# A decoder megakernel: the windowed attention's softmax in five plan steps instead of one

## The chip, the cores and the metric

The kernel is one program on one core of a Trainium2 chip. The metric is the device time of one execution in microseconds; lower is better.

## What is computed

The reference runs six blocks over x of 4 x 512 tokens with 256 channels: a time-mixing block, a quantised cross-attention, a mixture of experts, linear attention, cross-attention, and last a local-attention transformer of two layers. Only the last one's attention is touched. Cut to what matters:

```python
def _layer(x, wqkv, qs, ksc, wo, ...):
    qkv = shift_token(x) @ wqkv
    q, k, v = ...                      # 8 heads of 64
    q, k = rotary_xpos(l2norm(q) * qs, l2norm(k) * ksc)
    o = local_attention(q, k, v)       # a block of 128 queries sees its own
    x = x + o @ wo                     # and the previous block's 128 keys
    ...                                # then a gated feed-forward part

def local_attention(q, k, v):
    sim = einsum('bhwid,bhwjd->bhwij', bq * 8.0, bk)
    sim = where(mask, -max, sim)
    return einsum('bhwij,bhwjd->bhwid', softmax(sim), bv)
```

## The kernel before, in words

The tokens are 16 tiles of 128, four to a sequence. The windowed attention (`windowed_attention`) runs once per layer over 8 units of two tiles (u = 0 to 7, w = 0 or 1). One list of steps, `windowed_plan`, sets the order of the work: each engine's function (`attention_pe`, `attention_dve`, `attention_act`, `attention_pool`) walks the same list and issues its own part of each step, so the list gives the order in every engine's queue. Semaphores order the engines among each other. A step is named by kind, unit, tile, and for some the part.

For a tile the steps are: `project` (three products with the weights for queries, keys and values on TensorE, L3297; ScalarE empties the bank, L3505, and after the keys squares both, L3511; VectorE sums the squares, L3405), `split` (VectorE copies the shifted channels, L3396, ScalarE casts, L3493 and L3495, GpSimd subtracts, L3567; it prepares the input of a later unit's projections), `rotate` (VectorE L3422 and L3425 with GpSimd L3578 and L3579), `scale` (VectorE L3433, by the inverted norms), `invert` (ScalarE's square root L3515, VectorE L3409 and L3411), `turn` (TensorE's transposes L3306, ScalarE's copies L3524 for keys, L3529 for queries), `score` (L3318 writes the mask, L3325 the products, four banks for 8 heads), `softmax`, `flip` (transposes L3337 of the weights; ScalarE and VectorE copy one half each, L3480), `combine` (L3352, copied by ScalarE, L3553), `output` (L3362, added to x by VectorE, L3466).

The `softmax` step is one entry for three things. VectorE takes the maxima of heads 0 to 3 and 4 to 7 in two reductions (L3444) and scales each by -8 (L3446). ScalarE computes eight exponentials with sums (L3541), four after each half of the maxima. VectorE then, by halves, waits for the four exponentials, inverts their sums (L3452) and multiplies the weights (L3455, four heads). Whatever stands behind `softmax` in the list stands in VectorE's queue behind the last weights, and in ScalarE's behind the eighth exponential.

`mingle(main, side)` deals the entries of `side` evenly among those of `main`. In `windowed_plan` the main entries of unit u are the scores, softmaxes, flips, combines and outputs of its two tiles; the side entries are the rotations, scalings and turns of unit u + 1, mingled with the projections of unit u + 2 and the split of unit u + 3. So units 0 to 4 hold a split, units 0 to 5 projections, units 0 to 6 rotations; unit 7 has none of them. The first tile of units 0, 2, 4 and 6 opens a sequence (`alone`): it has one block of keys instead of two. The transposed and projected results share banks 4 to 7, given out in the order of the list (`m.banks`); the scores have banks 0 to 3. Two entries of the feed-forward part (`GATED_FIRST`) stand in units 6 and 7.

## Time and profile before

| | |
|---|---|
| time, median of 3 runs | 2578.68 us (2573.37 to 2583.72) |
| the profiled execution's own time | 2584.56 us |
| its span | 2583.2 us |
| TensorE busy | 2107.4 us, 82% of the span |
| VectorE busy | 1723.9 us, 67% |
| ScalarE busy | 1191.5 us, 46% |
| GpSimd busy | 872.3 us, 34% |
| mean granted TensorE clock | 0.906 of full |

The span runs from the first instruction to the last. PE is TensorE's matmuls, PEld its weight loads, DVE VectorE, ACT ScalarE, POOL GpSimd. Busy times are sums over the span; the rows further down give starts in us from the span's start, the duration, and in brackets the idle time before an instruction and what ended it. The first layer's windowed attention has its units 0 to 7 between some 1757 and 2026 us, the second's between some 2179 and 2446 us.

### The profile page before, as it was taken

Reading aid. Unit: us, or ns where it says so; the run is one execution under the profiler, and the core shown is the slowest. Engines: PE = TensorE matmul, PEld = TensorE weight load, DVE = VectorE, ACT = ScalarE, POOL = GpSimd, SP = SyncE. Lnnn points to the kernel's source line nnn. Section 1 sums busy time; section 2 is a strip of 40 time slices with the busy share of each in tenths; the row PEclk is TensorE's granted clock in tenths of the full one; section 3 lists DMA queues with packets and bytes.
Section 4 is the critical chain, followed back from the end, with each engine's and each line's share of the span. In section 5 each row is a group of like instructions: output and inputs, shape, how many; then the busy total and the mean of one; then the engine's idle time right before and its main releaser. Section 6 shows DMA issues by size and latency. Waiting matters only on the chain. (4 is left out here: it accounts for less than half of the span.)

```text
span 2583.2 us, 45827 instructions
## 1 busy us (share of the span) xinstructions
PE 2107.4 (82%) x17241; PEld 1348.7 (52%) x17241; DVE 1723.9 (67%) x3400; ACT 1191.5 (46%) x2208; POOL 872.3 (34%) x672
## 2 busy tenths in 40 slices
PE   5997579987589995887788989877787897787787
PEld 3554147874479993443344444444555554555544
DVE  4876977768966665666677777737677435777553
ACT  2132866646333332323245555445565434655552
POOL 2110024421056660012266767553221223221041
PEclk8998779999689997888899989988999998998999
DMA  4112024451351113222222322020000001000000
GB/s 145 44 49 53 1 82 132 135 171 55 128 220 50 51 46 125 76 82 89 76 75 72 94 70 70 22 76 34 1 1 1 25 1 51 1 1 1 33 9 25
DMA packets 107465, 159.63 MB, mean 62 GB/s; under 512 B 26064, under 2 KB 85236, under 8 KB 104180
## 3 DMA queue, kind: packets, MB, share of 16 engines
q1 hardware_dynamic: 102836, 144.64, 18.0%
q0 software_dynamic: 4416, 12.06, 1.6%
q8 instruction: 143, 2.34, 0.4%
q14 instruction: 70, 0.57, 0.1%
HBM read 109.42 MB, written 47.19 MB: 61 GB/s over the span
## 5 line engine op out<-in xcount | busy, mean ns | idle before, releaser
L2981 DVE TENSOR_REDUCE xa_max<-psum 128x1 f32<-128x1024 f32 (+1 forms) x256 | 246.4, 987 | 97.7 <-PE psum L2892 93.1
L3063 ACT ACTIVATE xa_work<-psum 128x1024 f32<-128x1024 f32 (+1 forms) x208 | 212.8, 1024 | 186.0 <-PE psum L2915 184.4
L3120 POOL TENSOR_TENSOR xa_ctx_f<-xa_ctx_f,xa_work 128x1024 f32<-128x1024 f32 x96 | 226.8, 2362 | 45.9 <-ACT xa_work L3063 37.9
L3297 PE MATMUL psum<-xa_c_parts,x_hl_f 128*128 128x512 bf16 x576 | 154.3, 417 | 63.3 <-ACT qk_raw_l L3505 24.8
L2892 PE MATMUL psum<-xa_key_rows,xa_query_rows 96*128 96x512 bf16 (+1 forms) x512 | 132.9, 352 | 36.9 <-DVE xa_max L2981 20.8
L1050 POOL TENSOR_TENSOR text_q<-text_q 128x512 bf16<-128x512 f32 x64 | 81.5, 1277 | 175.4 <-ACT text_q L1470 175.1
L2932 PE MATMUL psum<-xa_work,xa_values 128*32 128x128 f32 (+1 forms) x3328 | 140.7, 287 | 0.0
L2915 PE MATMUL psum<-xa_query_rows,xa_key_rows 98*128 98x512 bf16 (+1 forms) x416 | 130.3, 396 | 10.4 <-DVE xa_max L2981 10.4
L1802 PE MATMUL psum<-moe_rows,moe_w 128*128 128x256 bf16 x1104 | 130.4, 276 | 4.9 <-issue 4.9
L2061 ACT CAST x_ch<-moe_raw 128x512 bf16<-128x512 f32 x92 | 56.9, 618 | 158.7 <-DVE moe_raw L1976 158.2
L3297 PEld LDWEIGHTS psum<-xa_c_parts,x_hl_f 128*128 128x128 bf16 x576 | 56.3, 104 | 138.2 <-ACT qk_raw_l L3505 27.8
L1815 PE MATMUL psum<-moe_w,x_ch 128*128 x1104 | 124.1, 273 | 0.0
L3541 ACT ACTIVATE w_p_l<-psum,w_max_l 128x256 f32<-128x256 f32 (+1 forms) x256 | 110.6, 458 | 29.1 <-DVE w_max_l L3446 29.0
L2932 PEld LDWEIGHTS psum<-xa_work,xa_values 128*32 128x32 f32 (+1 forms) x3328 | 82.8, 112 | 75.0 <-issue 73.9
L1802 PEld LDWEIGHTS psum<-moe_rows,moe_w 128*128 x1104 | 109.0, 99 | 19.0 <-issue 5.5
L1815 PEld LDWEIGHTS psum<-moe_w,x_ch 128*128 128x128 bf16 x1104 | 108.0, 98 | 12.5
L1318 PE MATMUL psum<-ctx_f,probs_t 128*128 128x128 f32 (+1 forms) x832 | 103.7, 283 | 10.3 <-issue 5.3
L1318 PEld LDWEIGHTS psum<-ctx_f,probs_t 128*128 128x128 f32 (+1 forms) x832 | 99.2, 198 | 12.6 <-issue 5.7
L3809 POOL TENSOR_TENSOR hidden_f<-h_act_f,hidden_f 128x512 bf16<-128x512 f32 (+1 forms) x48 | 55.4, 1155 | 145.2 <-ACT hidden_f L3782 145.2
L2892 PEld LDWEIGHTS psum<-xa_key_rows,xa_query_rows 96*128 96x128 bf16 x512 | 43.1, 101 | 106.7 <-DVE xa_max L2981 31.6
L1976 DVE TENSOR_SCALAR moe_raw<-psum,cols 128x256 f32<-128x256 f32 x184 | 79.8, 477 | 22.1 <-PE psum L1802 17.1
L3730 DVE SCALAR_TENSOR_TENSOR h_act_f<-psum,cols,gelu_f 128x512 f32<-128x512 f32 (+1 forms) x48 | 35.7, 744 | 77.1 <-ACT gelu_f L3777 68.2
(482 smaller groups left out, 5118.7 us busy)
## 6 DMA issues: line engine op xcount, KB each, us to landing
text_q<-in_moe_w SPq DMA_DIRECT2D x64, 256.0 KB, 3.5
experts<-text_q SPq DMA_DIRECT2D x64, 256.0 KB, 2.8
moe_w<-experts SPq DMA_DIRECT2D x16, 1024.0 KB, 10.7
xa_key_rows<-cross_keys SPq DMA_DIRECT2D x48, 200.1 KB, 3.5
ctx_chunk<-in_ctxT SPq DMA_DIRECT2D x24, 300.0 KB, 3.0
cross_keys<-xa_k_hl SPq DMA_DIRECT2D x6, 800.5 KB, 3.7
moe_w<-pairs_out SPq DMA_DIRECT2D x8, 512.0 KB, 7.4
xa_ctx_f<-in_ctxT SPq DMA_DIRECT2D x4, 800.5 KB, 4.9
```

Source lines behind the costliest of these rows:

```text
L1050: g.tensor_tensor(parts[:, 1, :], t["expert_raw"][i % 2], parts[:, 0, :], ALU.subtract).then_inc(*s.e_low.up())
L1318: ins = pe.matmul(u.ap[:, 0:P], t["turned"][i % 2][0:rows, kt, :], t["values"][0:rows, n // TPB, kt, :], start=(kt == 0), stop=(kt == KT - 1))
L1802: ins = pe.matmul(u.ap[:, a * SLOT:(a + 1) * SLOT], w1[:, w, h, cf], t["x"][j % 2][:, x, h, :], start=(h, k) == (0, 0), stop=(h, k) == (1, 2))
L1815: ins = pe.matmul(u.ap[:, a * D:(a + 1) * D], t["hidden"][j % 2][:, x, f, q], w2[:, w, f, :], start=(f, k) == (0, 0), stop=(f, k) == (7, 2))
L2892: ins = pe.matmul(u.wide[:, x - c0:y - c0], t["q_rows"][n % 3][0:SPLIT, a, qt * P:(qt + 1) * P], t["k_rows"][n % 3][0:SPLIT, a, x:y], star ...
L2915: ins = pe.matmul(u.wide[0:rows, a * T:(a + 1) * T], t["k_rows"][n % 3][:, a, kt * P:kt * P + rows], t["q_rows"][n % 3][:, a, :], start=Tr ...
L2932: ins = pe.matmul(total.ap[lane:lane + NX, c:c + PIECE], t["v"][b][0:rows, kt, first + a, :], exps[0:rows, a, q:q + PIECE], start=(kt == 0 ...
L2981: v.tensor_reduce(t["maxes"][n % 2][:, qt * HU + a, part:part + 1], u.wide[:, 0:c1 - c0], AX.X, ALU.max).then_inc(*u.free)
L3063: act.activation(t["exps"][k % EXPS][0:rows], u.wide[0:rows].rearrange("p (m q) -> p m q", q=T), ACT.Exp, scale=1.0 / float(np.sqrt(np.flo ...
L3120: g.tensor_tensor(total, other, exps, ALU.add).then_inc(*s.added.up())
L3297: ins = pe.matmul(b.ap, x[:, i, h, w * P:(w + 1) * P], t["wqkv"][:, j, h, cols], start=(h, n) == (0, 0), stop=(h, n) == (1, 2))
L3541: ins = act.activation(t["p"][n % 2][:, i, lo:2 * P], scores[:, i, :], ACT.Exp, bias=t["peak"][n % 2][:, i:i + 1], scale=8.0, accum_out=t[ ...
```

## The change

One `softmax` entry becomes five: `peak` (both halves of the maxima, VectorE), `raise` for heads 0 to 3 and for 4 to 7 (ScalarE's exponentials), and `weigh` for the same halves (VectorE's reciprocal and weights). The previous tile's `combine` stands between the raises and the weighs. Since `mingle` counts entries, the side entries are dealt anew among all of them: 307 entries in the list instead of 243.

```diff
--- before.py
+++ after.py
@@ -3155,7 +3155,8 @@
                 before, after = GATED_FIRST[0:1], GATED_FIRST[1:2]
             elif n == LAST_W:
                 before = GATED_FIRST[2:3]
-            main += [("score", u, w)] + tail[0:1] + before + [("softmax", u, w)] + after + tail[1:2] + last
+            main += [("score", u, w)] + tail[0:1] + before + [("peak", u, w)] + [("raise", u, w, x) for x in range(2)] + after
+            main += tail[1:2] + [("weigh", u, w, x) for x in range(2)] + last
             last, tail = tail[2:], [("flip", u, w), ("combine", u, w), ("output", u, w)]
         rotations = rotate(u + 1) if u + 1 < UNITS_W else []
         projections = project(u + 2) if u + 2 < UNITS_W else []
@@ -3431,10 +3432,10 @@
             v.wait_ge(*s.added(n + 1))
             v.wait_ge(*s.inverted(u + 1))
             v.tensor_tensor(heads3(tn[:]), heads3(tn[:]), norm, ALU.mult).then_inc(*s.rotated.up())
-        elif kind == "softmax":
+        elif kind == "peak":
             w, = step[2:]
             n, lo = WU * u + w, alone(u, w) * P
-            peak, total, p = t["peak"][n % 2], t["total"][n % 2], t["p"][n % 2]
+            peak = t["peak"][n % 2]
             scores = m.psum[:, 0:4, :].rearrange("p b (x j) -> p (b x) j", x=2)[:, :, lo:2 * P]
             for x in range(2):
                 h = slice(4 * x, 4 * x + 4)
@@ -3446,14 +3447,16 @@
                 v.tensor_scalar(peak[:, h], peak[:, h], -8.0, None, ALU.mult).then_inc(*s.peaks.up())
             if n >= LAST_W - 2:
                 ffn_dve(m, fs, f, use, GATED_FIRST[n - LAST_W + 2:n - LAST_W + 3], layer)
-            for x in range(2):
-                h = slice(4 * x, 4 * x + 4)
-                v.wait_ge(*use["score", u, w, x].done)
-                v.reciprocal(total[:, h], total[:, h]).then_inc(*s.v_step.up())
-                v.wait_ge(*s.v_step.now())
-                for i in range(4 * x, 4 * x + 4):
-                    ins = v.tensor_scalar(p[:, i, lo:2 * P], p[:, i, lo:2 * P], total[:, i:i + 1], None, ALU.mult)
-                ins.then_inc(*s.weighed.up())
+        elif kind == "weigh":
+            w, x = step[2:]
+            n, lo, h = WU * u + w, alone(u, w) * P, slice(4 * x, 4 * x + 4)
+            total, p = t["total"][n % 2], t["p"][n % 2]
+            v.wait_ge(*use["score", u, w, x].done)
+            v.reciprocal(total[:, h], total[:, h]).then_inc(*s.v_step.up())
+            v.wait_ge(*s.v_step.now())
+            for i in range(4 * x, 4 * x + 4):
+                ins = v.tensor_scalar(p[:, i, lo:2 * P], p[:, i, lo:2 * P], total[:, i:i + 1], None, ALU.mult)
+            ins.then_inc(*s.weighed.up())
         elif kind == "flip":
             w, = step[2:]
             flip_out(m, t, use, u, w, 1)
@@ -3527,20 +3530,19 @@
                     act.wait_ge(*use["score", u - 2, WU - 1, 1].full)
                 act.wait_ge(*b.full)
                 act.copy(t["q"][u % 2][:, :, cols], view).then_inc(*b.free)
-        elif kind == "softmax":
-            w, = step[2:]
+        elif kind == "raise":
+            w, x = step[2:]
             n, lo = WU * u + w, alone(u, w) * P
             scores = m.psum[:, 0:4, :].rearrange("p b (x j) -> p (b x) j", x=2)[:, :, lo:2 * P]
-            if n > 1:
+            if n > 1 and x == 0:
                 before = (n - 2) // WU, (n - 2) % WU
                 act.wait_ge(*s.weighed(2 * (n - 1)))
                 act.wait_ge(*use[("flip",) + before + (len(flips(*before)) - 1,)].full)
-            for x in range(2):
-                act.wait_ge(*s.peaks(2 * n + x + 1))
-                for i in range(4 * x, 4 * x + 4):
-                    ins = act.activation(t["p"][n % 2][:, i, lo:2 * P], scores[:, i, :], ACT.Exp, bias=t["peak"][n % 2][:, i:i + 1],
-                                         scale=8.0, accum_out=t["total"][n % 2][:, i:i + 1])
-                ins.then_inc(*use["score", u, w, x].free)
+            act.wait_ge(*s.peaks(2 * n + x + 1))
+            for i in range(4 * x, 4 * x + 4):
+                ins = act.activation(t["p"][n % 2][:, i, lo:2 * P], scores[:, i, :], ACT.Exp, bias=t["peak"][n % 2][:, i:i + 1],
+                                     scale=8.0, accum_out=t["total"][n % 2][:, i:i + 1])
+            ins.then_inc(*use["score", u, w, x].free)
         elif kind == "flip":
             w, = step[2:]
             flip_out(m, t, use, u, w, 0)
```

Three places in the queues, all in unit 3 of the first layer (line numbers behind the change are one to three higher).

VectorE in the unit's first tile, before: the rotation of another tile (L3422, L3425), maxima, both halves' weights, then the sum of the squares (L3405).
```order
L3422 TENSOR_TENSOR qk_rot_l<-qk_raw_f,rotary_l 128x512
L3425 TENSOR_TENSOR qk_rot_l<-qk_rot_l,qk_other_l 128x512
L3444 TENSOR_REDUCE w_max_l<-psum 128x4
L3446 TENSOR_SCALAR w_max_l<-w_max_l 128x4
L3444 TENSOR_REDUCE w_max_l<-psum 128x4
L3446 TENSOR_SCALAR w_max_l<-w_max_l 128x4
L3452 RECIPROCAL w_sum_l<-w_sum_l 128x4
L3455 TENSOR_SCALAR w_p_l<-w_p_l,w_sum_l 128x256 x4
L3452 RECIPROCAL w_sum_l<-w_sum_l 128x4
L3455 TENSOR_SCALAR w_p_l<-w_p_l,w_sum_l 128x256 x4
L3405 TENSOR_REDUCE qk_norm_l<-qk_sq_f 128x16
```
And now, from the second half of the maxima on:
```order
L3445 TENSOR_REDUCE w_max_l<-psum 128x4
L3447 TENSOR_SCALAR w_max_l<-w_max_l 128x4
L3423 TENSOR_TENSOR qk_rot_l<-qk_raw_f,rotary_l 128x512
L3426 TENSOR_TENSOR qk_rot_l<-qk_rot_l,qk_other_l 128x512
L3406 TENSOR_REDUCE qk_norm_l<-qk_sq_f 128x16
L3434 TENSOR_TENSOR qk_rot_l<-qk_rot_l,qk_norm_l 128x512
L3455 RECIPROCAL w_sum_l<-w_sum_l 128x4
L3458 TENSOR_SCALAR w_p_l<-w_p_l,w_sum_l 128x256 x4
L3423 TENSOR_TENSOR qk_rot_l<-qk_raw_f,rotary_l 128x512
L3426 TENSOR_TENSOR qk_rot_l<-qk_rot_l,qk_other_l 128x512
L3455 RECIPROCAL w_sum_l<-w_sum_l 128x4
L3458 TENSOR_SCALAR w_p_l<-w_p_l,w_sum_l 128x256 x4
```
The rotation stands behind the maxima; the sum of the squares and a scaling stand ahead of the first weights, and one more rotation between the two halves.

VectorE in the unit's second tile, around the maxima. Before:
```order
L3395 MEMSET x_shifted_l 128x1
L3396 COPY x_shifted_l<-x_ch 128x255
L3444 TENSOR_REDUCE w_max_l<-psum 128x4
L3446 TENSOR_SCALAR w_max_l<-w_max_l 128x4
L3444 TENSOR_REDUCE w_max_l<-psum 128x4
L3446 TENSOR_SCALAR w_max_l<-w_max_l 128x4
```
Now:
```order
L3445 TENSOR_REDUCE w_max_l<-psum 128x4
L3447 TENSOR_SCALAR w_max_l<-w_max_l 128x4
L3445 TENSOR_REDUCE w_max_l<-psum 128x4
L3447 TENSOR_SCALAR w_max_l<-w_max_l 128x4
L3396 MEMSET x_shifted_l 128x1
L3397 COPY x_shifted_l<-x_ch 128x255
L3406 TENSOR_REDUCE qk_norm_l<-qk_sq_f 128x16
```
The shift's copy has moved from ahead of both maxima to behind them, and the sum of the squares follows it.

ScalarE in the same tile. Before:
```order
L3493 CAST x_hl_f<-x_ch 128x256
L3495 CAST x_hl_f<-x_shifted_l 128x256
L3529 COPY w_q_l<-psum 128x4x128
L3541 ACTIVATE w_p_l,w_sum_l<-psum,w_max_l 128x256 x8
L3505 COPY qk_raw_l<-psum 128x512
L3511 ACTIVATE qk_sq_f<-qk_raw_l 128x1024
```
Now:
```order
L3496 CAST x_hl_f<-x_ch 128x256
L3498 CAST x_hl_f<-x_shifted_l 128x256
L3543 ACTIVATE w_p_l,w_sum_l<-psum,w_max_l 128x256 x4
L3532 COPY w_q_l<-psum 128x4x128
L3543 ACTIVATE w_p_l,w_sum_l<-psum,w_max_l 128x256 x4
L3508 COPY qk_raw_l<-psum 128x512
L3514 ACTIVATE qk_sq_f<-qk_raw_l 128x1024
```
The cast of the shifted channels stays ahead of the exponentials; the queries' copy (`w_q_l`) stands between the two halves instead of ahead of both.

## Rows read from the trace of the kernel before

**Rows 1.** The page's first part: busy us (share of the span) and instructions.
```profile
PE 2107.4 (82%) x17241; PEld 1348.7 (52%) x17241; DVE 1723.9 (67%) x3400; ACT 1191.5 (46%) x2208; POOL 872.3 (34%) x672
```
**Rows 2.** Windows: us, then busy us (instructions) by engine, granted clock, DMA.
```profile
1859.50:1894.40 34.90, 28.68 (x226) 20.04 (x226) 25.34 (x52) 21.60 (x56) 7.82 (x10) 0.95 0.00 1
1962.90:1992.20 29.30, 19.00 (x147) 14.33 (x146) 22.09 (x55) 16.58 (x48) 3.76 (x4) 0.88 0.00 1
```
**Rows 3.** Waits over both stages: who for whom, us, times, longest us.
```profile
DVE w_sum_l L3452 <- ACT w_p_l L3541: 47.2, 54, 2.4
...
PE psum L3297 <- ACT qk_raw_l L3505: 24.8, 10, 2.7
...
PE psum L3297 <- ACT qk_raw_f L3505: 22.9, 8, 4.6
```
**Rows 4.** Timeline, unit 3, first tile: start us, us, engine, line, instruction.
```profile
1864.78 0.70 DVE L3422 TENSOR_TENSOR qk_rot_l<-qk_raw_f,rotary_l 128x512 f32<-128x512 f32 x1
...
1866.12 1.22 DVE L3444 TENSOR_REDUCE w_max_l<-psum 128x4 f32<-128x1024 f32 x1
...
1872.91 0.18 DVE L3452 RECIPROCAL w_sum_l<-w_sum_l 128x4 f32<-128x4 f32 x1 [0.47 <-ACT w_p_l L3541]
...
1873.12 1.14 DVE L3455 TENSOR_SCALAR w_p_l<-w_p_l,w_sum_l 128x256 f32<-128x256 f32 x4
...
1873.40 1.47 PE L3297 MATMUL psum<-xa_c_parts,x_hl_f 128*128 128x512 bf16 x6 [2.15 <-ACT qk_raw_l L3505]
...
1874.59 1.22 DVE L3405 TENSOR_REDUCE qk_norm_l<-qk_sq_f 128x16 f32<-128x1024 f32 x1 [0.33 <-ACT qk_sq_f L3511]
...
1882.05 1.21 DVE L3444 TENSOR_REDUCE w_max_l<-psum 128x4 f32<-128x1024 f32 x1
```
**Rows 5.** Group by line over both stages: count, busy us, mean ns, idle before.
```profile
L3433 DVE TENSOR_TENSOR qk_rot_l<-qk_rot_l,qk_norm_l 128x512 f32<-128x512 f32 x56 | 42.1, 754 | 1.1
```
**Rows 6.** Timeline, unit 3, second tile.
```profile
1881.85 0.29 DVE L3396 COPY x_shifted_l<-x_ch 128x255 f32<-128x255 f32 x1
...
1882.17 0.40 ACT L3495 CAST x_hl_f<-x_shifted_l 128x256 bf16<-128x256 f32 x1 [2.12 <-DVE x_shifted_l L3396]
...
1883.30 0.75 DVE L3446 TENSOR_SCALAR w_max_l<-w_max_l 128x4 f32<-128x4 f32 x1
...
1884.16 0.48 ACT L3541 ACTIVATE w_p_l<-psum,w_max_l 128x256 f32<-128x256 f32 x1 [1.10 <-DVE w_max_l L3446]
...
1887.78 0.63 ACT L3505 COPY qk_raw_l<-psum 128x512 f32<-128x512 f32 x1
...
1888.46 2.69 PE L3297 MATMUL psum<-xa_c_parts,x_hl_f 128*128 128x512 bf16 x6 [2.69 <-ACT qk_raw_l L3505]
...
1893.44 0.42 DVE L3466 TENSOR_TENSOR x_tok<-psum,x_tok 128x256 f32<-128x256 f32 x1 [2.65 <-PE psum L3362]
```
**Rows 7.** Timeline, unit 5, second tile's maxima.
```profile
1951.29 1.21 DVE L3444 TENSOR_REDUCE w_max_l<-psum 128x4 f32<-128x1024 f32 x1
...
1953.87 0.17 DVE L3446 TENSOR_SCALAR w_max_l<-w_max_l 128x4 f32<-128x4 f32 x1
```
**Rows 8.** Timeline, unit 6, a tile with half the keys, then its output.
```profile
1972.06 0.18 DVE L3452 RECIPROCAL w_sum_l<-w_sum_l 128x4 f32<-128x4 f32 x1 [2.13 <-ACT w_p_l L3541]
...
1972.27 0.87 DVE L3455 TENSOR_SCALAR w_p_l<-w_p_l,w_sum_l 128x128 f32<-128x128 f32 x4
...
1988.09 3.37 PE L3362 MATMUL psum<-wo_l,w_oc_l 128*128 128x256 f32 x8 [6.07 <-ACT w_q_l L3529]
```
**Rows 9.** Timeline, unit 0.
```profile
1767.81 1.06 ACT L3511 ACTIVATE qk_sq_f<-qk_raw_f 128x1024 f32<-128x1024 f32 x1
...
1779.10 1.22 DVE L3444 TENSOR_REDUCE w_max_l<-psum 128x4 f32<-128x1024 f32 x1
...
1786.37 2.77 PE L3297 MATMUL psum<-xa_c_parts,x_hl_f 128*128 128x512 bf16 x6
```
**Rows 10.** Window in unit 4, after a wait of TensorE.
```profile
1921.80:1925.40 3.60, 3.53 (x9) 1.89 (x10) 2.14 (x5) 3.11 (x6) 0.00 (x0) 0.50 0.00 0
```

## The prediction

> **What bounds the kernel now.** I read the page's busy shares first: TensorE is busy 82% of the span, VectorE 67%, ScalarE 46% [rows 1]. These are means over the whole program; the edit touches only the two windowed attention stages, so the windows by unit come next. A unit is two tiles of 128 tokens. In a middle unit of 34.9 us TensorE is busy 28.7, VectorE 25.3 and ScalarE 21.6; in unit 6, counted from 0, which has no projections left, it is 19.0, 22.1 and 16.6 of 29.3 [rows 2]. No engine is full, so the unit is a chain through all three. The waits say where it passes: over both layers VectorE waits 47.2 us in 54 waits for exponentials before it inverts their sums, and TensorE waits 24.8 + 22.9 us before projections for ScalarE's copy that empties a bank [rows 3]. The timeline of unit 3 ties them together: VectorE's maxima at 1866.12, eight exponentials, the projection's copy behind them in ScalarE's queue, and only then TensorE's projection at 1873.40, after 2.15 us of waiting [rows 4]; in the second tile the same with maxima at 1882.05 and the projection at 1888.46 after 2.69 us [rows 4, 6]. From there the path runs over output, transpose, ScalarE's copy and square root to VectorE's next unit.
>
> **The change part by part.** No instruction is added or dropped; TensorE's order changes in one or two places per unit (a transpose and the product with the values change places), and the count of table loads stays. What counts is the order on VectorE and ScalarE. I take a unit as the two stretches between the maxima.
>
> First tile of units 1 to 4. The rotation of another tile, which stood between the copies and the maxima, now follows the maxima. Its two instructions take 1864.78 to 1866.12, 1.34 us [rows 4], so maxima, exponentials, the copy, the squares and the projection behind them all come 1.34 us earlier. That is the gain, and it is what the TensorE wait of 2.15 us would like. But the weights (one reciprocal and four products, 0.18 + 1.14, about 1.3 us per half [rows 4]) now stand behind the norm reduction, which waits for the squares. Before, both halves were done by 1874.26, beside the exponentials; the stretch from the reduction's start at 1874.59 to the second tile's maxima at 1882.05 was 7.46 us without a pause [rows 4]. Now that stretch holds two weights more (+2.6) and the shift's copy less (0.29 long, some 0.2 of queue [rows 6]): 9.86 us. It begins 1.34 earlier. Second maxima: -1.34 + 2.6 - 0.2 = **+1.1 us**. In units 2 and 4 the first tile opens a sequence, has half the keys, and a half's weights take 0.18 + 0.87 = 1.05 us [rows 8]: -1.34 + 2.1 - 0.2 = **+0.6 us**. The rotation that fills VectorE's wait for the exponentials costs nothing there; what lost its cover are the weights.
>
> Second tile of units 1 to 4. ScalarE's split step casts what VectorE's shift copied. Before, the shift stood ahead of the maxima, and ScalarE had its cast (0.40) and a queries' copy done while it waited anyway [rows 6]. Now the shift follows both maxima, and ScalarE's cast stands ahead of the first four exponentials: these cannot start until both maxima are through. From the maxima's start to the projection on TensorE was 1888.46 - 1882.05 = 6.41 us [rows 4, 6]. Now: both maxima 1951.29 to 1954.04, 2.75 us [rows 7]; shift 0.29; cast 0.40; eight exponentials 1884.16 to 1887.78, 3.62; the queries' copy that is now dealt between the halves 0.46 (a copy of its size takes 0.63, an overlap of some 0.15 off); copy and release 1887.78 to 1888.46, 0.68 [rows 6]. Sum 8.20: **+1.8 us**. The weights again go behind the reduction, but here they fall into VectorE's wait for the output product (1.3 x 2 into 2.65 us [rows 6], and one for the square root follows), and the transposes that need them come after the next scores: nothing. Unit 1 or 3: +2.9; unit 2 or 4: +2.4; four units **+10.5 us**.
>
> In this sum the maxima take 2.75 us and not the 3.2 or so of unit 3. The scaling of the first maxima took 0.75 us there [rows 6] against 0.17 in unit 5 [rows 7]; in unit 3 GpSimd's rotations ran at that moment, and now they queue on GpSimd behind the split's subtraction, which waits for the cast, so they run later. The Trainium skill (SBUF — State Buffer, "Summary: rules for kernel authors") says that a VectorE operation in a two-port mode and a GpSimd operation block each other for the whole instruction; by it the change would take this block away, and without it each of eight units would be some 0.5 us dearer, 4 us more in all. The trace agrees in the size of the stretch, 0.75 against 0.17.
>
> Unit 5 has projections but no split. Its rotation already stood behind the copies; weights go behind the reduction, a scaling moves past the maxima, one copy goes between the halves: **+0.5 us**, bounded by -1 and +1.5.
>
> Unit 0 gains. Squares start at 1767.81 now [rows 9]; one scaling (0.75 at most, 0.6 in sequence [rows 5]) leaves from ahead of the maxima and one copy of 0.5 comes between the halves, so they start at 1767.7 and end 1.06 later. Then reduction 1.14, weights 2 x 1.05, scalings 2 x 0.62, rotations 2 x 1.34, one copy of the transposed weights, as large as a scaling, 0.6, make 7.8: maxima at 1776.6 instead of 1779.10. The projection follows 7.0 us later (2.75 + 0.62 + 0.29 + 0.40 + 0.46 + 1.81 + 0.68) at 1783.6 instead of 1786.37 [rows 9]: **-2.8 us**. Unit 6 has rotations and no projection, so the waits for exponentials are really filled: the first is 2.13 us [rows 8], and a scaling of 0.6 leaves from ahead of either tile's maxima: **-3.3 us**, with a shorter second wait left as margin, and the output product at 1988.09, after a wait of 6.07 us [rows 8], comes forward by this. Unit 7 keeps its order: nothing.
>
> Per layer 10.5 + 0.5 - 2.8 - 3.3 = +4.9, both layers **+10 us**. The profiled execution ran 2584.56 us for a span of 2583.2, 5.9 above the median of the three runs, 2578.68, so it is 2594 to 2595 for such an execution and **2589** against the median. About 0.5%, 12.9 us, is what a measurement of this kernel can tell from no change; the forecast is within it.
>
> Bounds: of the 1.8 us in the second tile, 0.5 could be saved if the queries' copy finds a gap, and 1.1 could be lost if the maxima stay as slow as in unit 3 and the shift loses its overlap; over eight tiles -4 to +9. The ends may give nothing (+12) or, with the waits' full size, 2 us more in each layer (-4). These hardly come together; this case reaches from 2579 to 2604.
>
> **The rivals.** *The exponentials' wait is filled and that is all (faster).* The edit means VectorE's 47.2 us and TensorE's 47.7 us of waits [rows 3]. If VectorE were the engine that sets the unit, each filled wait would count; half of 47.2 is 23.6: 2555 us. For it: unit 6, where VectorE is busy 22.1 of 29.3 us [rows 2]. Against it: in units 1 to 4 the reduction stands ahead of the weights and waits for squares that come after all eight exponentials, so the wait is moved and not filled. Chance 0.15.
>
> *Nothing reaches the path.* The later maxima are taken up by the waits that VectorE has before the output and the square root (2.65 us for the first in unit 3 [rows 6]), and the ends' gains too: 2579. Against it: those waits are themselves the end of the path from the projection, which starts later. Chance 0.15.
>
> *TensorE's clock (slower).* TensorE's wait before the second tile's projection grows from 2.69 to some 5 us in unit 3. After such a wait in unit 4 the granted clock was 0.50 over the next 3.6 us [rows 10], that is 1.2 of 2.4 GHz. In unit 3 the product after 2.69 us took 2.69 at a low clock too; after 6.07 us the output's eight matmuls took 3.37 [rows 8], and at double the pace they would take 1.7. If the low level lasts through projection and output in each of the eight middle units (1 to 4 of both layers), 1.5 us more each, 12 in all: 2601 us. It decides from the point where the output product in units 1 and 3 takes over 3 us. The Trainium skill (TensorE: Matmul & The Clock Gate, "What's actually happening") says that the throttled state is the default and that activity releases it; by it longer waits cost clock as well as time, and the rule speaks against this change. For it is the row of 0.50; against it, that both levels are in the times of before already. Chance 0.2.
>
> **How the numbers follow.** The forecast has 0.5, and it is the likeliest: 2589. Range: 2562 to 2604; below lies half and more of the faster rival, above the tail of the clock. Faster by over 0.5% (under 2565.8): most of the filled case, 0.14. Slower by over 0.5% (over 2591.6): a third of the forecast's own spread and nearly all of the clock, 0.36. Within: 0.5.
>
> **What would show it.** In the changed profile: second maxima in units 1 and 3 some 1 us later from the unit's start and the projection 3 us later; ScalarE's wait for the shift's copy larger by about 1 us per tile; the waits of the reciprocal for exponentials nearly gone and waits of the norm reduction for squares near 3 to 4 us in their place; units 1 to 4 of 36.5 to 38 us, units 0 and 6 shorter by 3. Middle units not longer than 35 us would make the forecast wrong, and ends that gain nothing would too.

## The result, and the profile after

The changed kernel ran 2590.47 us (median of 8 runs, 2586.39 to 2596.64); the kernel before, in the same comparison, 2573.40 us (8 runs, 2571.51 to 2583.72). The ratio is 1.0061, 95% interval 1.0043 to 1.0079: slower by 15.8 us, 11 to 20. The forecast was 2589.0 us, no more than 0.5% from before. The time was met within 1.5 us, and that is luck: its base had been 2578.68 us, the median of three runs, which eight runs put 5 us lower, and the difference came out 6 us larger than the +10 forecast, just on the far side of the 0.5%. One execution in the whole study, of e1 below, took 2742.91 us at a granted clock of 0.777, and medians and ratios leave it out.

The profiled execution ran 2586.39 us. Its page, first part, busy us and share of the span, and a window by `us, busy us (instructions) of PE, PEld, DVE, ACT, POOL, granted clock, DMA`, which is unit 3 of the first layer:

```profile
PE 2107.7 (82%) x17138; PEld 1353.9 (52%) x17241; DVE 1700.8 (66%) x3400; ACT 1188.7 (46%) x2208; POOL 860.3 (33%) x672
```
```profile
1853.35:1890.65 37.30, 28.78 (x223) 20.01 (x223) 24.12 (x52) 21.45 (x56) 6.88 (x10) 0.95 0.00 1
```

The shares are within one point of [rows 1] (PE's count is 103 lower because the trace lacks some matmuls; the weight loads are all there). Unit 3 is 37.30 us instead of 34.90 [rows 2], and no engine has more work in it than before, beyond 0.1 us; VectorE has 1.2 us less. The 2.4 us are idle time on all of them.

The two profiled spans, 2583.2 and 2585.1 us, differ by 1.9 us only, and that is no measure of the change. I cut each trace at ScalarE's square root of the norms, which opens a unit, and at the first gelu, which ends the stage. The two attention stages take 537.8 us before and 548.9 after, **+11.05 us**. All the rest, whose code is the same in both, took 2045.4 us in the one execution and 2036.2 in the other. In the twelve profiled executions of this study, each of another kernel, that rest lies anywhere between 2033.0 and 2045.4 us. So I read single profiles by their stages, and the whole time by medians.

Lengths in us, from square root to square root:

| | unit 0 | 1 | 2 | 3 | 4 | 5 | 6 and 7 | stage |
|---|---|---|---|---|---|---|---|---|
| before, first layer | 31.60 | 34.93 | 34.12 | 34.88 | 33.79 | 34.70 | 65.78 | 269.8 |
| after, first layer | 28.53 | 38.25 | 35.29 | 37.30 | 36.38 | 35.76 | 62.53 | 274.0 |
| before, second layer | 30.33 | 34.86 | 33.74 | 34.85 | 33.59 | 34.77 | 65.88 | 268.0 |
| after, second layer | 28.20 | 39.19 | 35.31 | 37.49 | 36.45 | 35.75 | 62.44 | 274.8 |

The waits over both stages (who for whom, us, times, longest), of the kernel after:

```profile
DVE qk_norm_l L3406 <- ACT qk_sq_f L3514: 122.5, 28, 6.2
...
ACT x_hl_f L3498 <- DVE x_shifted_l L3397: 59.0, 11, 7.3
...
PE psum L3307 <- ACT w_q_l L3532: 32.2, 10, 4.6
...
DVE w_sum_l L3455 <- ACT w_p_l L3543: 2.4, 6, 0.5
```

Three of them in the kernel before:

```profile
DVE w_sum_l L3452 <- ACT w_p_l L3541: 48.3, 56, 2.4
...
ACT x_hl_f L3495 <- DVE x_shifted_l L3396: 35.8, 13, 4.5
...
DVE qk_norm_l L3405 <- ACT qk_sq_f L3511: 20.6, 26, 3.4
```

The 48.3 us that VectorE waited for exponentials (47.2 over the slightly shorter stretch of [rows 3]) are down to 2.4, as the edit means them to be. In their place VectorE waits 122.5 us for squares, where before it waited 20.6. The wait has grown because what it waits for ends later than the exponentials, and because the weights, which used to fill that time, stand behind it now. The second line of the kernel after is the split's cast (35.8 us before), the third TensorE behind the queries' copy, which now stands between the two halves of the exponentials (12.9 us before).

Unit 3 of the kernel after shows both places. VectorE's timeline, first tile (start us, us, engine, line, instruction, in brackets the idle time before it and what ended it):

```profile
1853.61 0.18 DVE L3410 TENSOR_SCALAR qk_norm_l<-qk_norm_l 128x32 f32<-128x32 f32 x1 [2.10 <-ACT qk_norm_l L3518]
...
1857.41 1.21 DVE L3445 TENSOR_REDUCE w_max_l<-psum 128x4 f32<-128x1024 f32 x1
...
1860.83 0.69 DVE L3426 TENSOR_TENSOR qk_rot_l<-qk_rot_l,qk_other_l 128x512 f32<-128x512 f32 x1
1865.68 1.22 DVE L3406 TENSOR_REDUCE qk_norm_l<-qk_sq_f 128x16 f32<-128x1024 f32 x1 [4.16 <-ACT qk_sq_f L3514]
...
1867.62 1.14 DVE L3458 TENSOR_SCALAR w_p_l<-w_p_l,w_sum_l 128x256 f32<-128x256 f32 x4
...
1870.21 1.14 DVE L3458 TENSOR_SCALAR w_p_l<-w_p_l,w_sum_l 128x256 f32<-128x256 f32 x4
...
1875.33 1.21 DVE L3445 TENSOR_REDUCE w_max_l<-psum 128x4 f32<-128x1024 f32 x1
```

Counted from VectorE's first instruction of the unit, which was at 1861.09 before, the first maxima come at 3.80 us instead of 5.03 [rows 4]: the rotation's place is worth 1.23. The reduction comes at 12.07 instead of 13.50, after 4.16 us of idling, and then the stretch to the second maxima, with two lots of weights in it, is 9.65 us instead of 7.46. The second maxima are at 21.72 instead of 20.96.

The second tile of the same unit, in the timelines of VectorE, ScalarE and TensorE:

```profile
1876.58 0.17 DVE L3447 TENSOR_SCALAR w_max_l<-w_max_l 128x4 f32<-128x4 f32 x1
...
1878.00 0.29 DVE L3397 COPY x_shifted_l<-x_ch 128x255 f32<-128x255 f32 x1
...
1884.51 1.22 DVE L3406 TENSOR_REDUCE qk_norm_l<-qk_sq_f 128x16 f32<-128x1024 f32 x1 [6.22 <-ACT qk_sq_f L3514]
```
```profile
1878.32 0.40 ACT L3498 CAST x_hl_f<-x_shifted_l 128x256 bf16<-128x256 f32 x1 [4.93 <-DVE x_shifted_l L3397]
1878.63 0.47 ACT L3543 ACTIVATE w_p_l<-psum,w_max_l 128x256 f32<-128x256 f32 x1
...
1880.44 0.59 ACT L3532 COPY w_q_l<-psum 128x512 f32<-128x512 f32 x1
...
1882.71 0.63 ACT L3508 COPY qk_raw_l<-psum 128x512 f32<-128x512 f32 x1
```
```profile
1881.18 0.63 PE L3307 MATMUL psum<-const,qk_rot_l 128*128 128x128 f32 x4 [2.95 <-ACT w_q_l L3532]
1883.40 2.68 PE L3298 MATMUL psum<-xa_c_parts,x_hl_f 128*128 128x512 bf16 x6 [1.59 <-ACT qk_raw_l L3508]
1885.87 2.41 PE L3363 MATMUL psum<-wo_l,w_oc_l 128*128 128x256 f32 x8
```

Maxima at 1875.33, projection at 1883.40: 8.07 us, where it was 6.41 [rows 4, 6]. ScalarE starts its first exponential right behind the cast, and the cast right behind the shift, which stands behind both maxima. VectorE has nothing to do from the shift on and idles 6.22 us.

### The profile page after: what moved, and what is told of

Read it like the earlier page. It is cut to its first block and busy times, and to the rows that moved or that the text cites. A ratio compares the mean times of both kernels' runs of the same rounds, so it can differ in the third digit from the quotient of the medians.

```text
span 2585.1 us, 45724 instructions
## 1 busy us (share of the span) xinstructions
PE 2107.7 (82%) x17138; PEld 1353.9 (52%) x17241; DVE 1700.8 (66%) x3400; ACT 1188.7 (46%) x2208; POOL 860.3 (33%) x672
## 3 DMA queue, kind: packets, MB, share of 16 engines
q8 instruction: 143, 2.34, 0.4%
## 5 line engine op out<-in xcount | busy, mean ns | idle before, releaser
L2892 PE MATMUL psum<-xa_key_rows,xa_query_rows 96*128 96x512 bf16 (+1 forms) x512 | 131.6, 349 | 29.0 <-DVE xa_max L2981 13.7
L3406 DVE TENSOR_REDUCE qk_norm_l<-qk_sq_f 128x16 f32<-128x1024 f32 x32 | 39.0, 1219 | 125.7 <-ACT qk_sq_f L3514 125.7
L1802 PEld LDWEIGHTS psum<-moe_rows,moe_w 128*128 x1104 | 109.0, 99 | 18.8 <-issue 5.5
L3543 ACT ACTIVATE w_p_l<-psum,w_max_l 128x256 f32<-128x256 f32 (+1 forms) x256 | 111.0, 459 | 12.8 <-DVE w_max_l L3447 10.8
```

Of the source, the lines that this page charges most:

```text
L1802: ins = pe.matmul(u.ap[:, a * SLOT:(a + 1) * SLOT], w1[:, w, h, cf], t["x"][j % 2][:, x, h, :], start=(h, k) == (0, 0), stop=(h, k) == (1, 2))
L2892: ins = pe.matmul(u.wide[:, x - c0:y - c0], t["q_rows"][n % 3][0:SPLIT, a, qt * P:(qt + 1) * P], t["k_rows"][n % 3][0:SPLIT, a, x:y], star ...
L3543: ins = act.activation(t["p"][n % 2][:, i, lo:2 * P], scores[:, i, :], ACT.Exp, bias=t["peak"][n % 2][:, i:i + 1], scale=8.0, accum_out=t[ ...
```

## The experiments

Two kinds: from the changed kernel, one cost taken out again (e1, e2, e3); and from a kernel f0, which has the five kinds of step but the order of before, one cost or gain put in alone (f1, f2, f3). e4 has the new order at the ends only, and e5 and e6 look for something better than both. All measured against the kernel before:

| run | ratio, 95% | us by ratio | stages, us against before |
|---|---|---|---|
| after | 1.0061 (1.0043 to 1.0079) | +15.8 | +11.05 |
| f0 five together | 0.9984 (0.9969 to 0.9998) | -4 | -2.0 |
| e1 shift first | 0.9991 (0.9975 to 1.0007) | -2 | -3.0 |
| e2 weights first | 0.9895 (0.9873 to 0.9917) | -27 | -20.4 |
| e3 both | 0.9883 (0.9861 to 0.9906) | -30 | -33.5 |
| f1 reduction first | 1.0100 (1.0069 to 1.0130) | +26 | +25.0 |
| f2 shift late | 1.0046 (1.0031 to 1.0060) | +12 | +10.4 |
| f3 rotation in the wait | 0.9949 (0.9928 to 0.9969) | -13 | -13.7 |
| e4 ends only | 0.9973 (0.9955 to 0.9990) | -7 | -9.8 |
| e5 copy first | 0.9860 (0.9834 to 0.9885) | -36 | -39.5 |
| e6 projection first | 0.9803 (0.9772 to 0.9833) | -51 | -42.8 |

The third column is the ratio times some 2577 us, the last the two stages of one profile. They agree within 4 us in eight of the eleven rows, and within 8 in all. Against their base f0, whose stages are 2.0 us shorter than the kernel before's, f1, f2 and f3 have +26.9, +12.4 and -11.7 us.

For units 1 to 4 of both layers, eight units, I cut each unit once more, at ScalarE's squares of the second tile. The sums in us:

| run | start to second maxima | start to second squares | from there to the end | all |
|---|---|---|---|---|
| before | 163.2 | 214.5 | 60.2 | 274.8 |
| f0 | 163.7 | 215.0 | 59.2 | 274.1 |
| after | 168.3 | 233.0 | 62.6 | 295.7 |
| e1 | 169.5 | 224.7 | 57.0 | 281.8 |
| e2 | 145.3 | 210.1 | 63.0 | 273.1 |
| e3 | 146.4 | 201.6 | 58.7 | 260.2 |
| f1 | 181.6 | 232.8 | 55.8 | 288.6 |
| f2 | 160.6 | 221.6 | 62.1 | 283.7 |
| f3 | 151.7 | 203.0 | 57.1 | 260.1 |

The stretch up to the squares repeats from layer to layer within 0.1 us in half of the pairs; unit 2 is 0.3 us shorter in the second layer in every kernel, and e2's unit 1 is 1.1 us longer in it. So this stretch shows the order of the queues to some tenths of a us per unit.

The stretch behind the squares is the same work in every kernel of the table (projection, output, transpose, copy, square root) and still takes from 6.01 to 8.51 us. I cut it once more, at the end of the output product. From the projection's first weight load to there it is 3.67 to 6.16 us; the rest is 2.33 to 2.35 us in every one of the 72 units. All that varies is thus the time of these two products, and their work doesn't vary. The sums over the eight units: before 41.5 us, f0 40.4, after 43.9, e1 38.3, e2 44.2, e3 40.0, f1 37.1, f2 43.4, f3 38.4. I count from the weight load because in units 2 and 4 of some kernels, the kernel after among them, the trace lacks the first of the projection's six matmuls. The windows over the two products in unit 1 of the second layer, before and after, show TensorE's granted clock (the last figure but two) with the same 17 weight loads:

```profile
2239.77:2244.65 4.88, 4.88 (x16) 3.20 (x17) 2.08 (x5) 3.04 (x5) 0.00 (x0) 0.65 0.01 3
```
```profile
2235.86:2242.01 6.15, 6.15 (x16) 3.86 (x17) 3.67 (x11) 3.09 (x5) 0.00 (x0) 0.51 0.01 3
```

TensorE's two levels are 0.5 (1.2 GHz; the window of [rows 10]) and 1.0 (2.4 GHz; a window of f3 below); a figure in between means that the window holds some of each. The three kernels with the late shift (after, e2, f2) have the three longest sums, 2 to 4 us above their counterparts with the early one (e3 for e2, f0 and before for f2), and 5.6 in the pair of after and e1.

### f0: five steps, old order

```diff
-            main += [("score", u, w)] + tail[0:1] + before + [("peak", u, w)] + [("raise", u, w, x) for x in range(2)] + after
-            main += tail[1:2] + [("weigh", u, w, x) for x in range(2)] + last
+            main += [("score", u, w)] + tail[0:1] + before + [("softmax", u, w)] + after + tail[1:2] + last
...
+        if step[0] == "softmax":
+            u, w = step[1:]
+            plan += [("peak", u, w)] + [("raise", u, w, x) for x in range(2)] + [("weigh", u, w, x) for x in range(2)]
```

> Five steps, but placed one after another where the one softmax entry stood, so that every queue has the order of before. Theory (only the order counts): the time of before, ratio 1.000 within 0.3%. Rival (the split into steps itself costs, by another order of waits or another program): some of the 15.8 us of the change stay, ratio above 1.003.

Measured: 2574.54 us, ratio 0.9984; stages 535.9 us against 537.8. Splitting the entry costs nothing; what the change costs is all in the new dealing. The same order of the queues, profiled twice, thus gives stages that differ by 2.0 us, 1.5 of them in the first layer's unit 0 (30.13 us for 31.60). f0 is therefore the base for f1 to f3.

### e1: the changed kernel, shift ahead of the second tile's maxima

```diff
-    return plan + last + tail
+    plan += last + tail
+    for u in range(3, UNITS_W):
+        at, to = plan.index(("split", u)), plan.index(("peak", u - 3, 1))
+        if at > to:
+            plan.insert(to, plan.pop(at))
+    return plan
```

> The change, with the split step ahead of the second tile's maxima again. Theory (ScalarE's cast waits for a shift that stands behind both maxima): in units 1 to 4 the stretch from the second maxima to the projection falls from 8.07 us by 1.3, the median by some 10 us against the change, to about 1.002 of before. Rival (the shift is hidden; the loss is the weights' or the clock's): no change against the change, 1.006.

Measured: 2574.38 us, ratio 0.9991; the stages are 14.1 us shorter than in the kernel after, 13.9 of them in units 1 to 4. By the table 8.3 us lie ahead of the second squares, 1.0 per unit, and 5.6 behind, all of these in projection and output (38.3 us for 43.9). From the second maxima to the squares e1 takes 6.90 us, after 8.09, before 6.43: of the change's 1.66, 1.19 are the shift and its cast, and the 0.47 that stay are the queries' copy between the exponentials.

### e2: the changed kernel, weights ahead of the norm reduction

```diff
+def dve_order(plan):
+    plan = list(plan)
+    for u in range(2, UNITS_W):
+        for w in range(WU):
+            at, to = plan.index(("project", u, w, 1)), plan.index(("weigh", u - 2, w, 1))
+            if at < to:
+                plan.insert(to, plan.pop(at))
+    return plan
...
-    for step in plan:
+    for step in dve_order(plan):
```

VectorE alone walks the rearranged list; the other engines' queues stay as they are.

> The change, with VectorE's sum of the squares behind both halves of the weights instead of ahead of the first; the shift stays behind the maxima. Theory (the weights lost their cover because they stand behind a wait for the squares): VectorE's wait of 4.16 us in the first tile goes to under 1, the second maxima of a middle unit come 2 to 3 us earlier, eight such units give 16 to 24 us, ratio 0.997 to 1.000 of before. Rival (TensorE's queue sets the second maxima, the weights have room): under 4 us gained, ratio about 1.005. By the clock rival a gain of the wait alone, with the output product unchanged.

Measured: 2553.18 us, ratio 0.9895; the stages are 31.5 us shorter than after, more than expected. 22.6 lie in units 1 to 4 and 8.6 in the two units 5, which go from 35.76 and 35.75 us to 31.42 and 31.52. The second maxima come 2.9 to 3.0 us earlier in seven of the eight middle units (19.09 us from the start in unit 3, for 21.98), and from them to the squares it is 8.09 us as in the kernel after: the cost of the weights lies wholly in the first tile. It is more than the weights' length of 2.6 and 2.1, because the edit also puts a scaling and a rotation, which stood behind the reduction, into the wait: in unit 3 the reduction starts 13.13 us behind VectorE's first instruction instead of 12.07, and the stretch from there to the maxima falls from 9.65 to 5.70. So the order of reduction and weights is the largest cost in the change, and it reaches unit 5, where I had looked for little.

### e3: both

> Both of the last two edits on the change. Theory: the two costs are on one path and add up, 26 to 34 us less than the change, some 10 to 18 us under before, ratio 0.993 to 0.996, with what the change gained left over: rotation inside the wait for exponentials and the ends' 3 us each. Rival (they hide each other): no better than the better of the two alone, ratio 0.998 or more.

Measured: 2548.44 us, ratio 0.9883, beyond the expected range on the fast side. The stages lose 44.6 us against after; e1 and e2 alone lose 14.1 and 31.5, 45.6 together. The two costs add up within 1 us. Unit 3's VectorE timeline in e3:

```profile
1858.63 0.18 DVE L3470 RECIPROCAL w_sum_l<-w_sum_l 128x4 f32<-128x4 f32 x1
...
1862.13 1.14 DVE L3473 TENSOR_SCALAR w_p_l<-w_p_l,w_sum_l 128x256 f32<-128x256 f32 x4
...
1863.19 1.21 DVE L3421 TENSOR_REDUCE qk_norm_l<-qk_sq_f 128x16 f32<-128x1024 f32 x1
...
1868.89 0.28 DVE L3412 COPY x_shifted_l<-x_ch 128x255 f32<-128x255 f32 x1
...
1869.10 1.21 DVE L3460 TENSOR_REDUCE w_max_l<-psum 128x4 f32<-128x1024 f32 x1
1870.34 0.73 DVE L3462 TENSOR_SCALAR w_max_l<-w_max_l 128x4 f32<-128x4 f32 x1
```

No bracket from the weights to the second maxima: the exponentials and squares are there when VectorE comes to them, because other work stands in between. The maxima at 1869.10 are 19.05 us behind the unit's first VectorE instruction, against 20.96 before and 21.72 after.

### f1: old order, reduction ahead of the weights

```diff
+            at, to = plan.index(("project", u, w, 1)), plan.index(("weigh", u - 2, w, 0))
+            if at > to:
+                plan.insert(to, plan.pop(at))
```

(again in VectorE's order only)

> The order of before, with one thing moved: VectorE's sum of the squares ahead of both halves of the weights in units 0 to 5. Theory (this is what takes the weights' cover away): in the first tile the wait for the squares holds both weights, 2 x 1.3 us later second maxima less what the removed waits of 2.0 + 0.5 us had already held: 2.5 us per unit, in ten to twelve units 20 to 28 us, ratio 1.008 to 1.011. Rival (only together with the rotation's move or the shift does it cost): ratio 1.000 to 1.003.

Measured: 2602.58 us, ratio 1.0100; stages +25.0 us, as expected: 13.9 in units 1 to 4, 8.8 in the units 5 (3.2 and 5.6), 3.1 in the units 0, and 0.8 less in units 6 and 7. Up to the second squares the middle units take 18.3 us more (2.9 each in units 1 and 3; 1.8 in 2 and 4, one of them 1.4), behind them 4.4 less, again all in the two products. Nothing else is changed here. Its waits:

```profile
DVE qk_norm_l L3422 <- ACT qk_sq_f L3530: 125.9, 30, 6.0
...
DVE w_sum_l L3471 <- ACT w_p_l L3559: 6.9, 8, 2.1
```

These are nearly the figures of the kernel after, without any rotation in the wait and without the new dealing. **That the waits for exponentials disappear is thus no sign of a gain:** here they do so in the slowest kernel of the study.

### f2: old order, shift behind the second tile's maxima

```diff
+    for u in range(3, UNITS_W):
+        at, to = plan.index(("split", u)), plan.index(("peak", u - 3, 1))
+        plan.insert(to, plan.pop(at))
```

> The order of before, with one thing moved: the split step behind the second tile's maxima in units 0 to 4. Theory: exponentials start after both maxima, shift and cast instead of after the first maxima, 1.3 us per unit, ten units 10 to 13 us, ratio 1.004 to 1.005, all of it in the wait of ScalarE for the shift. Rival (it costs only where the queries' copy is dealt between the halves too): 1.000.

Measured: 2584.86 us, ratio 1.0046; stages +10.4 us, as expected, 9.0 of them in units 1 to 4. But only 7.0 of these lie up to the squares, 0.9 per unit for the 1.3 expected; 1.9 are the two products behind them. The group of the scaling of the maxima (count, busy us, mean ns, idle before), first f2, then before:

```profile
L3456 DVE TENSOR_SCALAR w_max_l<-w_max_l 128x4 f32<-128x4 f32 x64 | 12.9, 201 | 2.2
```
```profile
L3446 DVE TENSOR_SCALAR w_max_l<-w_max_l 128x4 f32<-128x4 f32 x64 | 18.6, 290 | 2.2
```

The late shift by itself takes 89 ns off the mean of the 64 scalings.

### f3: old order, rotation behind the first tile's maxima

```diff
+    for u in range(1, UNITS_W):
+        at, to = plan.index(("rotate", u, 0, 1)), plan.index(("peak", u - 1, 0))
+        if at < to:
+            plan.insert(to, plan.pop(at))
```

> The order of before, with one thing moved: the rotation that stands ahead of the first tile's maxima goes behind them, ahead of the weights, in units 0 to 6. Theory (VectorE's waits for exponentials are on the path and the rotation fits into them): 1.34 us per unit where it stood ahead of the maxima, units 1 to 4, and where it stood behind the weights, units 0, 5 and 6, 1.3 us too: 14 x 1.3 = 18 us at most, ratio 0.993 to 0.996. Rival (nothing reaches the path): 1.000.

Measured: 2563.15 us, ratio 0.9949; stages -13.7 us. I had expected 1.3 us in every unit; it is 2.7 to 2.8 in units 1 and 3, 0.8 to 1.0 in units 2 and 4, and nothing in 0, 5 and 6, where it had been expected too. The 2.7 is more than the two instructions last. TensorE's timeline in unit 3 of f3, and the window over it:

```profile
1871.78 1.47 PE L3304 MATMUL psum<-xa_c_parts,x_hl_f 128*128 128x512 bf16 x6 [2.67 <-ACT qk_raw_l L3523]
1873.48 1.96 PE L3369 MATMUL psum<-wo_l,w_oc_l 128*128 128x256 f32 x8 [0.23 <-ACT w_k_l L3542]
```
```profile
1871.70:1875.40 3.70, 3.39 (x16) 2.20 (x17) 2.15 (x5) 3.02 (x6) 0.00 (x0) 1.00 0.00 0
```

and the same two products in the kernel before and after, each in one window:

```profile
1888.40:1893.30 4.90, 4.84 (x16) 3.03 (x17) 2.13 (x5) 3.09 (x6) 0.00 (x0) 0.65 0.00 0
```
```profile
1883.30:1888.20 4.90, 4.80 (x15) 3.00 (x16) 3.62 (x11) 3.13 (x6) 0.00 (x0) 0.65 0.00 0
```

The wait ahead is the same, 2.67 us here and 2.69 before [rows 6], but the granted clock is 1.00 and not 0.65, and projection and output take 3.66 us from the first's start to the second's end instead of 4.88. That is 1.2 of the 2.7. The table says it for all: up to the squares f3 gains 11.5 us in eight units, 1.3 to 1.5 in each, which is the rotation; behind them the stretch falls from 7.2 to 6.01 us in units 1 and 3 and grows by some 0.5 in 2 and 4, 3.1 less together, which is what projection and output take less (38.4 us for 41.5). So the rotation's place is worth what the prediction said, and where the stretch behind it comes out short, it is by TensorE's clock.

### e4: new dealing in units 0, 6 and 7, old in 1 to 5

```diff
+            if 0 < u < UNITS_W - 2:
+                main += [("score", u, w)] + tail[0:1] + before + [("softmax", u, w)] + after + tail[1:2] + last
+            else:
...
```

> The new dealing in units 0, 6 and 7 only, the order of before in units 1 to 5. Theory: the ends gain 3.1 to 3.3 us each per layer as in the profile of the change and nothing is lost between: 12 us, ratio 0.995. Rival (the ends' gains are given back in the units that follow, unit 1 above all, which grew most in the change): ratio 0.998 or more, with unit 1 longer than 35 us.

Measured: 2567.21 us, ratio 0.9973 (0.9955 to 0.9990), short of the 0.995 expected and not at the rival's 0.998 either; stages -9.8 us, in units 0 (-3.3 and -1.8) and 6 with 7 (-2.5 and -2.7). Unit 1 is 34.93 us in the first layer, as before: what the ends gain isn't given back by the next unit, and the 38.25 us of the kernel after are unit 1's own.

### e5: e3, and the queries' copy ahead of the second tile's exponentials

```diff
+    for u in range(1, UNITS_W):
+        at, to = plan.index(("turn", u, 0, 0)), plan.index(("raise", u - 1, 1, 0))
+        if at > to:
+            plan.insert(to, plan.pop(at))
```

> The change with both edits (split ahead of the maxima, sum of the squares behind the weights) and ScalarE's copy of the queries ahead of the first four exponentials again. Theory (the copy dealt between the halves delays the second half and TensorE's transposes, which waited 30.5 us for it in the version with both edits): 0.5 us per unit, 4 to 8 us less than with both edits, ratio 0.985 to 0.987 of before. Rival (the projection's copy behind the eighth exponential sets the path all the same, the copy only fills): under 2 us, ratio 0.988.

Measured: 2538.80 us, ratio 0.9860; stages -6.0 us against e3, as expected, 5.2 of them in units 1 to 4 and 4.4 of these up to the squares.

### e6: e5, and ScalarE's copy and squares of the projection ahead of them too

```diff
+def act_order(plan):
+    plan = list(plan)
+    for u in range(2, UNITS_W):
+        at, to = plan.index(("project", u, 1, 1)), plan.index(("raise", u - 2, 1, 0))
+        if at > to:
+            plan.insert(to, plan.pop(at))
+    return plan
```

> As the last one, and in the second tile ScalarE takes the keys' projection with its squares ahead of the exponentials instead of behind them, in units 0 to 5. Theory (TensorE's last projection of a unit waits for a bank that this copy empties, and that is how the exponentials get onto the path to the next unit): the copy comes some 4 us earlier, the exponentials 0.6 to 1.6 us later, 2 to 3 us less per unit, 20 to 30 us under the last one, ratio 0.975 to 0.980 of before. Rival (weights and their transposes come next and bound the unit at once, or ScalarE waits for the projection): under 8 us, ratio 0.983 or more.

Measured: 2526.74 us (2518.14 to 2541.68), ratio 0.9803 (0.9772 to 0.9833): faster than before by some 51 us, and the best version of the study. Against e5 that is 15 us by the ratios, under the 20 to 30 expected, and the stages give only 3.3 us of it, which is the rival's "under 8": the middle units gain 1.2 us in all eight, and not 2 to 3 in each. The profiled execution is the slowest of the four (2541.68 us at a mean granted clock of 0.910; the others 2518.14 to 2527.68 at 0.915 to 0.917), so its stages may not stand for the others. Its interval and e5's (0.9834 to 0.9885) all but touch. How much this last step brings is open. The waits of the profiled execution:

```profile
PE psum L3372 <- ACT w_oc_l L3583: 35.1, 14, 3.8
...
DVE w_sum_l L3474 <- ACT w_p_l L3571: 22.1, 30, 2.1
DVE qk_norm_l L3425 <- ACT qk_sq_f L3542: 14.0, 6, 3.4
```

The output product waits 35.1 us for the copy of its operand, 4.9 us in the kernel after: that copy stands behind all eight exponentials in ScalarE's queue. It is the next place to look at.

## Why the prediction was right, and where it was not

**Whole.** The sum was +9.8 us, unrounded; the stages show +11.05, and the medians 15.8 with an interval that begins at 11. The mechanism is the one forecast: two dependences, each moved to where it is waited for, against a rotation moved to where it is covered. The sum is closer than its parts: in the middle units 2.4 us too much and 2.4 us that were left out cancel, and the time itself owes its 1.5 us to a base that was 5 us too high. The 5 us between stages and medians are in no row that I can name; a rest of the program that varies by 12 us between executions can make them, but that isn't shown. A forecast of 0.4% lay close to the bound of 0.5%, and "slower", where the result fell, deserved about as much as "within"; it had 0.36 against 0.5.

**By places.**

| | forecast | measured in the stages |
|---|---|---|
| units 1 to 4, both layers | +21 | +20.9 |
| unit 5, both | +1.0 | +2.0 |
| unit 0, both | -5.6 | -5.2 |
| units 6 and 7, both | -6.6 | -6.7 |

**By terms**, for the eight middle units, us up to the second squares, where the order of the queues decides:

| | forecast | measured |
|---|---|---|
| rotation behind the maxima | -10.7 | -11.5 (f3) |
| weights behind the reduction | +18.8 | +18.3 (f1) |
| shift, cast and copy, less the shift's 0.2 | +12.8 | +12.1 (e1: 8.3 and 8 x 0.47) |
| sum | +20.9 | +18.9; in the kernel after +18.5 |
| behind the squares | 0 | +2.4 |

- *First tile.* Each piece is right within 1 us over eight units, but the split of the weights is not: 2.9 in units 1 and 3 for 2.6, 1.4 to 1.8 in units 2 and 4 for 2.1. In unit 3 the reduction is 1.43 us earlier for 1.34, the stretch to the maxima 9.65 us for 9.86. The second maxima are +0.76 for the forecast's +1.1, in units 2 and 4 +0.45 (once +0.11) for +0.6.
- *Second tile.* From maxima to projection 8.07 us for 8.20, that is +1.66 for +1.8, and the 0.46 for the copy that was dealt between the halves is 0.47. "Here they fall into VectorE's wait for the output product": right, e2 takes nothing off this stretch.
- *Behind the squares: the step that was missing.* The +20.9 of the middle units is met because +2.4 us, to which the forecast gave nothing, stand where the queues gave 2.4 less; that is luck. All of the 2.4 lies in projection and output, which take 43.9 us in the eight units instead of 41.5, at TensorE's clock; what follows them is 2.34 us in both kernels. It is the rival's mechanism at a fifth of its size.
- *Unit 5, +0.5.* Measured +1.06 and +0.98, inside the bounds, but the term is not small: the reduction's place costs 4.3 us there (e2) and the rest of the new dealing brings 3.3 (31.42 against 34.70 before). It was a guess at the net of two terms that were not worked out.
- *Ends.* In unit 0 the second maxima were put 16.4 us behind the unit's start (1776.6) and came at 16.22, the projection 7.0 behind them and came at 6.84. The rows, unit 0's projection and unit 6's output in the kernel after:

```profile
1774.34 2.74 PE L3298 MATMUL psum<-xa_c_parts,x_hl_f 128*128 128x512 bf16 x6 [1.13 <-ACT qk_raw_f L3508]
...
1984.66 2.55 PE L3363 MATMUL psum<-wo_l,w_oc_l 128*128 128x256 f32 x8 [3.96 <-ACT w_q_l L3532]
```

The output's wait of 6.07 us [rows 8] is 3.96, and the product starts 21.87 us into unit 6 instead of 23.89. e4, with the ends alone, gains 9.8 us of the 12: they depend a little on what the middle does. And 1.5 us of the 5.2 in unit 0 isn't sure, since f0, with the queues of before, has 30.13 us there for the 31.60 of the kernel before.
- *The signs.* Middle units of 36.5 to 38 us: units 3 and 4 lie there or a tenth below, unit 1 above (38.25 and 39.19), unit 2 below (35.3). The reduction's waits are 4.4 us in the mean, for 3 to 4. ScalarE's wait for the shift grew by more than the 1 us per tile, from 2.8 to 5.4 us in the mean: what is longer there was idle anyway.

**The maxima at 2.75 us.** The scaling's 0.75 us [rows 6] was expected to fall to 0.17 with GpSimd's rotations out of its way. It did: the group of the kernel after has a mean of 171 ns over all 64, against 290.

```profile
L3447 DVE TENSOR_SCALAR w_max_l<-w_max_l 128x4 f32<-128x4 f32 x64 | 10.9, 171 | 2.2
```

In e3, with the shift first again, the 0.73 us are back (1870.34 above). The Trainium skill (SBUF — State Buffer, "Summary: rules for kernel authors") has VectorE's two-port modes and GpSimd block each other for a whole instruction. The traces agree: in all twelve, each of the 465 scalings that start while no GpSimd instruction runs takes 0.17 us. The 303 others take 0.17 to 0.75, and each ends 0.01 us or more behind the GpSimd instruction that was running, so those that start at its end lose nothing. It is a gain of 7.7 us of VectorE's busy time, bought with a shift whose place costs more.

**The rivals.** *The filled wait* falls: the wait is gone and the time is not. It is the experiments' clearest point, since f1 removes the same wait and is slower by 1%; e2 and e3 show that the idea was sound and only the reduction's place spoilt it, and the 2555 us that this rival gave are close to what e2 and e3 reach. *Nothing reaches the path* falls with +20.9 us in the middle units. *TensorE's clock* falls in size: its deciding point, the output product of units 1 and 3 over 3 us, came true in unit 1 (3.29 and 3.62 us) and not in unit 3 (2.41 and 2.53). But unit 1's took 3.23 us in the first layer before, too, and the two products are 2.4 us longer in eight units, for the 12 of the rival. Nor did the one wait ahead of the projection grow to 5 us: it is 1.59 us in unit 3, behind another of 2.95 for the queries' copy. The Trainium skill's rule (TensorE: Matmul & The Clock Gate, "What's actually happening"), that activity releases the clock, would have made longer waits dearer. The traces agree in the sign for the late shift (2.4 us more here, and the three longest sums of the table) and not for f1, whose middle units are 1.7 us longer than before with the same work, so that TensorE idles more, and whose two products take 4.4 us less. Between the units it goes both ways: the two products take 0.9 and 1.3 us more than before in unit 1, 1.0 and 0.6 less in unit 2, 0.0 and 0.2 more in unit 3, 0.8 and 0.7 more in unit 4. So unit 1 grew by 3.3 and 4.3 us and unit 2 by 1.2 and 1.6, where I had forecast 2.9 and 2.4.

## What to carry to other kernels

In a queue that runs strictly in order, a wait is filled only if the instruction that stands behind it needs something that is ready sooner than what the wait is for; putting ready weights behind a reduction that waits for later squares moves the wait and lengthens it. When a list of steps is dealt anew, look at each engine's order for pairs in which the one that becomes ready later now stands first, and mend those by hand. Here two such pairs are more than all of the loss: the same new dealing without them is 1.2% faster than before, 1.4% with a third mended (e5), and some 2.0% with a fourth (e6, whose share is open). Judge by the stretch to the engine that is waited for, not by the waits that vanish.

## What the runs showed of the hardware

- After waits of equal length (2.69 us before, 2.67 in f3) the same product took 2.69 us in a window with a granted clock of 0.65 and 1.47 us in one with 1.00. The wait's length alone doesn't tell which level follows; what does is open. It isn't chance either: in units 1 and 3 of both layers projection and output took 3.67 or 3.68 us each time in f1 and f3, and 4.87 to 4.95 before. These two products are all that moves the stretch behind the squares between 6.01 and 8.51 us.
- A scaling of 128 x 4 took 0.17 us with no GpSimd instruction beside it, 465 times of 465, and up to 0.75 us beside one.
- The same code outside the two stages took 2033.0 to 2045.4 us in the twelve profiled executions, a spread as large as the whole effect of the change. Two profiles alone would have told "+1.9 us".
